# Layer 1's mixture of experts: answers written by indexed DMA to the token's places, plain loads and GpSimd sums in the last stage

## What is computed

```
x1 = _layernorm(x + attn_out, g1, be1)
topk_p, topk_i = jax.lax.top_k(softmax(x1 @ Wg + bg), 2);  topk_p = topk_p / sum(topk_p)
h = gelu(x1 @ W1[e] + b1[e]);  y[e] = h @ W2[e] + b2[e]        # 8 experts, 128 -> 512 -> 128
moe_out = sum over the two experts of topk_p * y[expert]
return _layernorm(x1 + moe_out, g2, be2)                       # and x = x + this
```

## Time and profile before

| | us |
|---|---|
| median of 3 runs | 2486.95 (2485.18 to 2489.42) |
| profiled execution, time | 2488.63 |
| profiled execution, span | 2486.8 |
| PE busy in the span | 2028.1 (82%) |
| DVE busy | 1989.5 (80%) |
| ACT busy | 1537.1 (62%) |
| POOL busy | 562.4 (23%) |

### The profile page before, as it was taken

The page is one execution under the profiler, slowest core; times in us unless marked ns, Lnnn a source line. Parts: engine busy times, 40 slices in busy tenths (PEclk is TensorE's granted clock), DMA queues, the critical chain, the costliest instruction groups (busy, mean ns, idle before and its releaser), DMA issues. The chain is left out here.

```text
span 2486.8 us, 45503 instructions
## 1 busy us (share of the span) xinstructions
PE 2028.1 (82%) x16896; PEld 955.6 (38%) x16896; DVE 1989.5 (80%) x3274; ACT 1537.1 (62%) x3022; POOL 562.4 (23%) x686
## 2 busy tenths in 40 slices
PE   6999775882689999999998769999999999459920
PEld 5888564661312222222222312222222222349920
DVE  7888557666879999999993779999999995476636
ACT  5554330342329989989897519988989889106510
POOL 2444300767410000000000320000000000306455
PEclk9999975895759999999999769999999999559965
DMA  5000010344521111011100441010110100302212
GB/s 195 1 1 1 1 42 1 85 89 128 160 58 33 33 30 34 24 38 28 34 6 15 137 124 33 19 43 21 32 42 21 41 7 10 124 4 74 68 53 58
DMA packets 94412, 121.16 MB, mean 49 GB/s; under 512 B 23665, under 2 KB 56561, under 8 KB 93937
## 3 DMA queue, kind: packets, MB, share of 16 engines
q1 hardware_dynamic: 73712, 78.92, 11.4%
q0 software_dynamic: 8960, 18.37, 3.3%
q10 hardware_dynamic: 11520, 20.98, 2.7%
HBM read 69.70 MB, written 42.99 MB: 45 GB/s over the span
## 5 line engine op out<-in xcount | busy, mean ns | idle before, releaser
L1549 DVE TENSOR_REDUCE mx<-psum 128x1 f32<-128x1024 f32 x1024 | 1174.7, 1214 | 76.8 <-PE psum L1437 75.8
L1526 ACT ACTIVATE p<-psum 128x512 f32<-128x512 f32 x2048 | 1102.4, 596 | 108.5 <-PE psum L1459 66.6
L1471 PE MATMUL psum<-p,v_ext 128*32 128x256 f32 x8192 | 656.3, 392 | 39.3 <-ACT p L1526 39.2
L1437 PE MATMUL psum<-ks,qs 64*128 64x512 bf16 x2048 | 635.9, 395 | 53.3 <-DVE mx L1549 29.7
L1459 PE MATMUL psum<-qs,ks 64*128 64x512 bf16 x2048 | 630.4, 383 | 1.5 <-ACT p L1526 1.3
L1471 PEld LDWEIGHTS psum<-p,v_ext 128*32 128x32 f32 x8192 | 162.0, 108 | 473.9 <-ACT p L1526 254.3
L1459 PEld LDWEIGHTS psum<-qs,ks 64*128 64x128 bf16 x2048 | 123.8, 93 | 404.1 <-ACT p L1526 367.8
L1339 POOL CAST m_near<-mx 128x16 bf16<-128x16 f32 x128 | 25.3, 197 | 1079.6 <-DVE mx L1549 1075.5
L759 ACT ACTIVATE hid<-psum,stage 128x128 f32<-128x128 f32 x448 | 132.5, 367 | 178.0 <-PE psum L729 178.0
L703 POOL DMA_INDIRECT x_in<-n_rows,token_of x152 | 153.7, 1011 | 296.8 <-POOLq L85 219.6
L1437 PEld LDWEIGHTS psum<-ks,qs 64*128 64x128 bf16 x2048 | 118.9, 94 | 115.5 <-DVE mx L1549 81.0
(11 more groups left out here) (244 smaller groups left out, 2145.1 us busy)
## 6 DMA issues: line engine op xcount, KB each, us to landing
qs<-qk_parts SPq DMA_DIRECT2D x128, 104.0 KB
ks<-qk_parts SPq DMA_DIRECT2D x128, 104.0 KB
qk_parts<-piece__1 ACTq DMA_DIRECT2D x40, 256.0 KB, 3.8
qk_parts<-piece__2 ACTq DMA_DIRECT2D x40, 256.0 KB, 3.4
answers<-y_out SPq DMA_DIRECT2D x152, 64.0 KB, 1.5
ew<-in_moe SPq DMA_DIRECT2D x1, 5136.0 KB, 18.8
ew<-in_moe SPq DMA_DIRECT2D x1, 4624.0 KB, 14.1
n_rows<-n_all SPq DMA_DIRECT2D x8, 512.0 KB, 3.2
```

The costliest lines, as they stand in the source:

```text
L1437: pe.matmul(psum[:, bank, :], a["qs"][r, g % NKF, j % KM, i * P:(i + 1) * P], a["ks"][r, g % NKF, j % KM, k * HALF:(k + 1) * HALF], start= ...
L1471: last = pe.matmul(psum[GR * j:GR * j + VW, O_BANK, q], t["v_ext"][:, b * NT + i, VE * (h0 + j):VE * (h0 + j) + VW], a["p"][:, (GH * s + j ...
L1526: act.activation(a["p"][:, n % NP, :], psum[:, S_BANK + n % NS, :], ACT.Exp, scale=DH ** -0.5)\
L1549: dve.tensor_reduce(a["mx"][:, g % 2, h, j, 0, c:c + 1], psum[:, bank:bank + 2, :].rearrange("p a c -> p (a c)"), AX.X, ALU.max)\
```

## The change

In layer 1, each answer goes straight to its token's place. The constants `token` now number the pairs: token + 1 for the first choice, token + 1 + 4096 for the second, so `invert` yields the pair's number of each slot. VectorE works out two index columns from it: `token_of` (both layers) for the gather, and in layer 1 `place_of` for the write. Padding slots get places of their own behind the 8192 (`spare`). In `expert_tiles` of layer 1, SP's stores are gone, and GpSimd issues an indexed write of each `y_out` to `pair_answers`, in the order gather(i), scatter(i - 5). In layer 0, SP stores as before.

In `finish`, SP loads a batch's two answers with two plain DMAs of 512 KB (`load`), the first two batches at the stage's head, the others behind the stores of the batch two before. GpSimd has no DMA left; it takes scale, shift and last sum, by halves of a batch (128x512 each), with `x2` in two copies. VectorE waits, from the third batch on, for the sums of the batch two before. The second sum of `combine` reads the first from `mixed` as before.

```diff
@@ constants @@
-                ("token", B * NT)):
+                ("token", 2 * B * NT), ("spare", 72)):
-                        ("token", 1 + P * np.arange(B * NT) + r[:, None])):
+                        ("token", 1 + P * (np.arange(2 * B * NT) // 2) + B * L * (np.arange(2 * B * NT) % 2) + r[:, None]),
+                        ("spare", 1 + 2 * B * L + P * np.arange(72) + r[:, None])):
@@ invert @@
-            link(dve.tensor_scalar(t["token_f"][:, 0:tiles], psum[:, 2, 0:tiles], -1.0, 0.0, ALU.add, ALU.max))
-            dve.tensor_copy(t["token_of"][:, 0:tiles], t["token_f"][:, 0:tiles])
+            of, token, place = t["pair_f"][:, 0:tiles], t["token_f"][:, 0:tiles], t["place_f"][:, 0:tiles]
+            link(dve.tensor_copy(of, psum[:, 2, 0:tiles]))
+            link(dve.tensor_scalar(token, of, B * L + 0.5, -float(B * L), ALU.is_gt, ALU.mult))
+            link(dve.scalar_tensor_tensor(token, token, -1.0, of, ALU.add, ALU.add))
+            dve.tensor_scalar(t["token_of"][:, 0:tiles], token, 0.0, None, ALU.max)
+            if layer:
+                link(dve.scalar_tensor_tensor(place, of, 0.0, t["spare"][:, 0:tiles], ALU.is_equal, ALU.mult))
+                dve.scalar_tensor_tensor(t["place_of"][:, 0:tiles], place, -1.0, of, ALU.add, ALU.add)
@@ expert_tiles @@
+    NX, NST, AHEAD = PLACES, 3, 5
+            def scatter(i):
+                pool.wait_ge(y_ready, i + 1)
+                pool.indirect_dma_start(t["pair_answers"],
+                                        bass.IndirectOffsetOnAxis(ap=t["place_of"][:, i:i + 1], axis=0),
+                                        t["y_out"][:, i % NX, :], None).then_inc(stored[i % NX], 16)
+
+            for i in range(tiles + AHEAD):
+                if i < tiles:
+                    gather(i)
+                if layer and i >= AHEAD:
+                    scatter(i - AHEAD)
@@ finish @@
+            def load(b):
+                if b >= 2:
+                    sp.wait_ge(mixed, 2 * NT * (b - 1))
+                for k in range(2):
+                    r = B * L * k + L * b
+                    sp.dma_start(t["back"][:, b % 2, k, :, :], t["pair_answers"][r:r + L, :].rearrange("(i p) d -> p i d", p=P))\
+                        .then_inc(loaded[b % 2], 16)
...
             for b in range(B):
-                if b >= 2:
-                    pool.wait_ge(mixed, 2 * NT * (b - 1))
-                fetch(pool, t, b)
+                for h in range(NH):
+                    pool.wait_ge(normed, NT * b + TPH * (h + 1))
+                    pool.tensor_tensor(x2[b % 2][:, s, :], x2[b % 2][:, s, :], row("g2"), ALU.mult).then_inc(scaled, 1)
+                    pool.wait_ge(scaled, n)
+                    pool.tensor_tensor(x2[b % 2][:, s, :], x2[b % 2][:, s, :], row("be2"), ALU.add).then_inc(shifted, 1)
+                    pool.wait_ge(shifted, n)
+                    pool.tensor_tensor(x[b](h * TPH, TPH), x[b](h * TPH, TPH), x2[b % 2][:, s, :], ALU.add)\
+                        .then_inc(added, 1)
...
-                link(dve.tensor_tensor(x2[:, :, :], x2[:, :, :], t["row"]("g2"), ALU.mult))
-                link(dve.tensor_tensor(x2[:, :, :], x2[:, :, :], t["row"]("be2"), ALU.add))
-                for h in range(NH):
-                    dve.tensor_tensor(x[b](h * TPH, TPH), x[b](h * TPH, TPH), x2[:, h * TPH:(h + 1) * TPH, :],
-                                      ALU.add).then_inc(added, 1)
```

More of the change, by code:

```diff
@@ L643, in floor, with invert @@
     link(dve.tensor_scalar(x, x, -float(3 * 2 ** 22), None, ALU.add))
-def invert(nc, t, tiles):
+def invert(nc, t, layer, tiles):
     psum, T = t["psum"], B * NT
@@ L688, in expert_tiles @@
     B2 = B1 + F
-    NX, NST = PLACES, 3
+    NX, NST, AHEAD = PLACES, 3, 5
     with stage(nc, "staged", "turned", "x_ready", "hidden", "activated", "y_done", "y_ready",
@@ L699, in _, with gather @@
             pool.wait_ge(t["n_stored"], 16 * B * (layer + 1))
-            for i in range(tiles):
+            def gather(i):
                 if i >= NX:
@@ L705, in _ @@
                     .then_inc(gathered[i % NX], 16)
[L707 to L713, removed]
+            def scatter(i):
[8 more added lines that the diff above has]
+                    scatter(i - AHEAD)
+            if layer:
+                for i in range(tiles - NX, tiles):
+                    pool.wait_ge(stored[i % NX], 16 * (i // NX + 1))
+        if not layer:
+            @block.sync
+            def _(sp):
+                for i in range(tiles):
+                    sp.wait_ge(y_ready, i + 1)
+                    sp.dma_start(t["answers"][i * P:(i + 1) * P, :], t["y_out"][:, i % NX, :])\
+                        .then_inc(stored[i % NX], 16)
+                for i in range(tiles - NX, tiles):
+                    sp.wait_ge(stored[i % NX], 16 * (i // NX + 1))
         @block.tensor
@@ L942, in finish @@
 def finish(nc, t, x, n):
-    xn, x2 = t["xn"], t["x2"]
-    with stage(nc, "mixed", "step", "var_ready", "std_ready", "normed", "added") as \
-            (block, mixed, step, var_ready, std_ready, normed, added):
+    xn, x2 = t["xn"], (t["x2"], t["x2_b"])
+    with stage(nc, "mixed", "step", "var_ready", "std_ready", "normed", "scaled", "shifted", "added",
+               "loaded0", "loaded1") as \
+            (block, mixed, step, var_ready, std_ready, normed, scaled, shifted, added, *loaded):
         @block.sync
         def _(sp):
+            def load(b):
[5 more added lines that the diff above has]
+                        .then_inc(loaded[b % 2], 16)
+            load(0)
+            load(1)
             for b in range(B):
@@ L954, in _ @@
                         .then_inc(t["out_stored"], 16)
+                if b + 2 < B:
+                    load(b + 2)
             sp.wait_ge(t["out_stored"], 16 * NH * B)
@@ L959, in _ @@
             for b in range(B):
-                if b >= 2:
-                    pool.wait_ge(mixed, 2 * NT * (b - 1))
-                fetch(pool, t, b)
+                for h in range(NH):
+                    s = slice(h * TPH, (h + 1) * TPH)
+                    row = lambda name: t["row"](name)[:, s, :]
+                    n = NH * b + h + 1
+                    pool.wait_ge(normed, NT * b + TPH * (h + 1))
[5 more added lines that the diff above has]
+                        .then_inc(added, 1)
         @block.scalar
@@ L973, in _ @@
             for b in range(B):
[L974 to L977, removed]
-                link(dve.tensor_tensor(x2[:, :, :], x2[:, :, :], t["row"]("g2"), ALU.mult))
-                link(dve.tensor_tensor(x2[:, :, :], x2[:, :, :], t["row"]("be2"), ALU.add))
-                for h in range(NH):
-                    dve.tensor_tensor(x[b](h * TPH, TPH), x[b](h * TPH, TPH), x2[:, h * TPH:(h + 1) * TPH, :],
-                                      ALU.add).then_inc(added, 1)
+                dve.wait_ge(loaded[b % 2], 16 * 2 * (b // 2 + 1))
+                for i in range(NT):
+                    dve.scalar_tensor_tensor(t["mixed"][:, i, :], t["back"][:, b % 2, 0, i, :], t["wt"][:, b * NT + i, 0:1],
+                                             n[b](i, 1).rearrange("p a d -> p (a d)"), ALU.mult, ALU.add).then_inc(mixed, 1)
+                for i in range(NT):
+                    dve.wait_ge(mixed, 2 * NT * b + i + 1)
+                    dve.scalar_tensor_tensor(xn[:, i, :], t["back"][:, b % 2, 1, i, :], t["wt"][:, b * NT + i, 1:2],
+                                             t["mixed"][:, i, :], ALU.mult, ALU.add).then_inc(mixed, 1)
+                dve.wait_ge(mixed, 2 * NT * (b + 1))
+                if b >= 2:
+                    dve.wait_ge(added, NH * (b - 1))
+                norm_steps(dve, t, link, (var_ready, std_ready, normed), b, xn, x2[b % 2])
 def wait_for_pair(eng, t, layer, pair):
@@ L1607, in build @@
         t["answers"] = nc.dram_tensor("answers", [SLOT_TILES * P, D], F32).ap()
+        t["pair_answers"] = nc.dram_tensor("pair_answers", [2 * B * L + 72 * P, D], F32).ap()
         t["slot_of"] = sb("slot_of", [P, B * NT, 2], U32)
@@ L1696, in mixture @@
                 t["lo_hot"], t["hi_hot"] = sb("lo_hot", [P, 2, INV, P], where=scope), sb("hi_hot", [P, 2 * INV, tiles], where=scope)
-                t["token_f"] = sb("token_f", [P, tiles], where=scope)
-                t["token_of"] = sb("token_of", [P, tiles], U32, where=scope)
+                for name in ("pair_f", "token_f", "place_f"):
+                    t[name] = sb(name, [P, tiles], where=scope)
+                t["token_of"], t["place_of"] = (sb(name, [P, tiles], U32, where=scope) for name in ("token_of", "place_of"))
                 for name in ("x_in", "y_out"):
@@ L1708, in mixture @@
                 route(nc, t, layer, E, tiles)
-                invert(nc, t, tiles)
+                invert(nc, t, layer, tiles)
                 expert_tiles(nc, t, layer, tiles, F, func)
@@ L1751, in build @@
         with ExitStack() as scope:
-            t["back"] = sb("back", [P, 2, NT, 2, D], where=scope)
```

(3 more changed lines are left out.)

2 lines of the change are left out of this document (1 added, 1 removed).

## The result

| | before | after |
|---|---|---|
| median, us | 2486.3 (2485.18 to 2489.42, 4 runs) | 2523.22 (2522.32 to 2524.03, 4 runs) |
| profiled execution, time / span | 2488.63 / 2486.8 | 2524.03 / 2522.2 |
| first gather of layer 1 | 2232.33 | 2234.31 |
| start of `finish` | 2379.1 | 2446.40 |
| length of `finish` | 107.7 | 75.8 |

The change makes the kernel slower: ratio 1.0145, 95% interval 1.0129 to 1.0161, 36.9 us between the medians and 35.4 between the spans. The forecast was 2494, its range ended at 2512. `finish` gives 31.9 us back (39.1 expected), and the expert tiles of layer 1 with the inverse table and the seam behind them take 67.3 more (46.0 expected). The seam is the stretch from the last tile's work to the first load of `finish`. A pair is one gather and one scatter on GpSimd, from one gather's start to the next one's.

What follows compares the result with a forecast made beforehand. Bounds taken: TensorE in layer 1's expert tiles, GpSimd's 64 indexed reads in `finish`. Expert tiles +44.7, inverse table +1.3, `finish` -39.1 make +6.9 us on 2486.95: 2494, range 2478 to 2512.

Steps and rivals of the forecast that it cites:

- 65.5 pairs: Layer 1's expert tiles: from first scatter to last gather, GpSimd needs 2.60 us a pair, against TensorE's 1.90 a tile.
- last gather to last scatter: End of layer 1's expert tiles: 2.66 us to the last tile's turn, 5.7 us from turn to answer.
- last scatter to `finish`: After layer 1's expert tiles: the last scatter lands in 2.6 us, the next stage begins 0.9 us later.
- three batches: `finish`: VectorE's 10.3 us a batch plus 4 x 1.0 lost to GpSimd's sums, 14.3 us each.
- rival D: Layer 1's expert tiles: TensorE falls to 1.2 GHz in the gaps, 4.3 us a tile, toward 2600 us; chance 0.03.
- the weight copy's price: Layer 1's expert tiles: VectorE's 0.76 us weight copy delays GpSimd's descriptor writes, raising a pair from 2.50 to 2.60 us.
- rival B: Layer 1's expert tiles: the weight copy falls into every pair, 3.12 us each, 34 us more, 2528 us; chance 0.10.
- The upper bound of the range: Slow ends together: pairs of 2.75 us (+54.6), inverse table +1.3, `finish` -32.3, so +23.6 us, 2511.
- two of six sums would fit beside the statistics: `finish`: two of GpSimd's six instructions a batch run beside statistics and reciprocal (2.9 us), so only four delay VectorE.
- all held up: `finish`, slow bound: all six GpSimd instructions delay VectorE, batches of 16.3 us, the stage 75.4 us, -32.3.
- Rival A: `finish`: port sharing costs nothing, VectorE keeps GpSimd out, which sums beside statistics; 2482.4 us, or 2476; chance 0.25.
- Those of 2 and 3 come in time: `finish`: plain loads of batches 2 and 3 wait at SP behind the stores, yet delay nothing.

Runs made afterwards that it cites:

- tiny_copy_2: Changed kernel, but from layer 1's fourth tile VectorE copies one column of a tile's weights instead of 1156 (stale weights), second set: 2507.7 us.
- norm_act: Changed kernel, but in `finish` ScalarE normalises, eight activations a batch, and GpSimd keeps scale, shift and sum: 2512.72 us, ratio 1.0095 to the kernel before.
- repair: Changed kernel, but ScalarE copies layer 1's weights and normalises in `finish`, VectorE does the sums one batch behind: 2502.6 us, ratio 1.0057 to the kernel before.
- tiny_copy: Same edit to the changed kernel as tiny_copy_2, on the first set's chip: 2571.64 us, where the kernel before took 2531.44.
- act_copy: Changed kernel, but ScalarE copies layer 1's tile weights instead of VectorE, first set: 2569.01 us, ratio 1.0151 to the kernel before.

## Why the prediction was wrong

By its own steps, in spans, forecast 2493.7 and measured 2522.2, 28.5 apart:

| step | forecast | measured | off |
|---|---|---|---|
| first scatter (inverse table in it) | 2243.0 | 2243.64 | +0.6 |
| 65.5 pairs | 2.60 each | 2.84 each | +15.7 |
| last gather to last scatter | 8.3 | 9.68 | +1.4 |
| last scatter to `finish` | 3.5 | 7.05 | +3.5 |
| first loads | 6.0 | 5.8 | -0.2 |
| first batch | 11.3 | 13.3 | +2.0 |
| three batches | 14.3 each | 16.5 each | +6.6 |
| sums left, last store, end | 8.4 | 7.1 | -1.3 |

Right: the change of the bound to GpSimd, the indexed write at the read's price (0.99 and 0.30), answers ready and places free in time, the clock (rival D falls for this kernel: 1.00 from 2250 to 2440), the first loads, and that VectorE's batches do not stay at 10.3.

**The step that failed is the weight copy's price, 0.10 us a pair.** It was 0.27, shown by tiny_copy_2. The undisturbed pair is 2.566, 0.07 above the 2.50 of the forecast, so of the 0.24 by which a pair is off, 0.17 is the copy and 0.07 the two instructions themselves. I had spread the loss of a free-running train (instructions back to back) over its 9.4 copies, as if copies fell anywhere in it, and had put beside it the 0.03 of the earlier trace rows. Both hide that the price hangs on the phase, which is the distance from the gather's start to the copy's. In the changed kernel turn, answer and copy follow the gather, so the copy comes near a gather's start in nearly every pair: of the 66 gathers, 54 are longer than 1.05 us. The rows, copy against gather: 1.54 long with the copy 0.06 us ahead, 1.50 with 0.10 ahead (2307.04 and 2307.14 above), 1.20 with 0.41 ahead; 1.06 with it 0.18 behind, 1.37 with 0.49 behind. A copy that starts with the gather costs it nothing, and one more than 0.55 behind nothing either:

```profile
2396.38 0.96 POOL L709 DMA_INDIRECT x_in<-n_rows,token_of  x1 [0.30 <-issue]
2396.43 0.76 DVE L807 COPY stage<-ew 128x1156 f32 x1
```

The earlier trace rows has the copy 0.09 us behind the gather's start, so its 0.03 is the price of that one phase. Another phase stood in the same trace of the kernel before, 45 us earlier:

```profile
2255.09 0.76 DVE L784 COPY stage<-ew 128x1156 f32 x1
2255.17 1.50 POOL L703 DMA_INDIRECT x_in<-n_rows,token_of  x1 [0.30 <-issue]
```

A scatter is lengthened in nine of 72 cases. That is rival B's mechanism, which I gave a chance of 0.10, at under half its price: 0.27 us a pair for the copy instead of 0.62. The phase moves from pair to pair and is seldom the worst one. B's 0.62 came from a gather that met two copies (2235.71 and 2236.83). The upper bound of the range had the pair at 2.75, which no row supported. With the measured 2.84 it would be 2516, with B's 3.12 it would be 2535; from 2516 to the measured 2523 it is mostly the seam and the last tile in front of it.

**The second is that two of six sums would fit beside the statistics.** None does. A batch is 10.3 + 3.1 + 3.1 = 16.5: all six are met, the "all held up" bound (75.4, measured 75.8). The same paragraph had said where they go: three into L203 of their own batch, three into the next combining. L203 of the first half's tiles releases three sums at once, the last L203 the other three, and VectorE is in a train of the instructions that collide at both moments. To let two through, something had to delay them, and nothing does. Against each of the six VectorE got one instruction through.

The Trainium skill ("SBUF — State Buffer", section "Who interferes with whom") says that the pair of ports goes to whoever issues first, for the whole instruction. The rows of L203 (5.25), L1020 (5.33) and norm_act's product of 8 columns (1.19) agree with it. The same section of the Trainium skill says that a VectorE instruction with a single input in SBUF, outside the two-port modes, doesn't contend with GpSimd. The statistics beside norm_act's sums (1.65) agree with that.

**The third is the seam.** The forecast put 3.5 us from the last scatter to `finish`: the landing of an indexed read, and the 0.9 that follow the landing of a plain store. It is 7.05 us. A scatter lands in 2.2 us by its issue row, so with the 0.9 some 3.9 us have no row. 1.5 of them go when SP waits in GpSimd's place; the cause of the other 2.4 is open.

Rival A is no rival but half a truth: in norm_act VectorE's train does keep a sum out for 2.3 us. In the changed kernel the sums start where VectorE's own instruction releases them, and the two take turns. What decides between taking turns and keeping out was not tried apart. "Those of 2 and 3 come in time" was right only because the batches were long: as soon as they fell to 8 to 12 us, the loads cost 12.2 us (repair).

## What to carry to other kernels

An instruction that disturbs a train does not fall into it at random when the train feeds it: work out its phase, and take the price of the locked phase as the bound of the range. Work moved from VectorE to GpSimd is a gain only if it meets instructions that GpSimd doesn't hold up; here six sums spared 3.7 us of VectorE and cost it 6.2. An idle share of an engine in a stage (0.93 of 1.90 us) is worth what it hides: what stands out of it, 2.84 - 1.90 = 0.94 us, some 66 times, is 62 us, about twice the 31.9 that `finish` gives back.

## What the runs showed of the hardware

- An indexed write of 128 rows of 512 B takes GpSimd 0.99 us and 0.30 of issue, as much as the indexed read (0.97 and 0.30), and lands in 2.2 us.
- A VectorE copy of 0.76 us makes an indexed read up to 0.57 longer (1.54). The price hangs on the phase: it is highest with the copy just ahead of the read's start, and nothing where both start within 0.05 us. The same copy by ScalarE, 1.18 us long, adds nothing (0.97).
- Between GpSimd sums of 1.26 back to back one VectorE instruction gets through for each, at 128x128 as at 128x8: eight normalising instructions go from 2.15 to 5.25 us, a product of 8 columns from 0.17 to 1.19.
- From last answer to first load stand 7.62 us behind indexed writes and 2.84 behind plain stores.
- On the chip of the first set, tiny_copy and act_copy show a gap of TensorE in every third tile and nine stretches with its clock at 1.2 GHz, some 41 us of the stage. In the changed kernel and on the chips of the other two sets the clock stays at 2.4 GHz from the stage's first 10 us to its last tile.
